# Class token's keys and values folded into the rounds of a patch tokenizer; attention 0's QKV tiles directly behind them

## What is computed

```python
red = grid.mean(axis=(3, 5))                      # 9 windows, 9 patches in each
q = _ln(red, la_ln_q_g, la_ln_q_b) @ la_wq
kv = _ln(win, la_ln_kv_g, la_ln_kv_b) @ la_wkv
local_out = red + softmax(q k) v @ la_proj_w + la_proj_b
gq = _ln(cls, ga_ln_q_g, ga_ln_q_b) @ ga_wq       # class token
gkv = _ln(local_out, ga_ln_kv_g, ga_ln_kv_b) @ ga_wkv
cls_out = cls + softmax(gq gk) gv @ ga_proj_w + ga_proj_b
patch_out = local_out @ mod_w + mod_b
h = concatenate([patch_out, cls_out])             # 10 tokens
h = h + attention_0(_layernorm(h))                # 16 heads of 16, all 10 tokens
```

## Time and profile before

| | us |
|---|---|
| median of three runs | 892.69 |
| lowest and highest | 891.36, 897.75 |
| the profiled execution, its own time | 895.31 |
| its span from first to last instruction | 893.6 |
| PE busy | 744.4 (83%) |
| DVE busy | 572.6 (64%) |
| POOL busy | 383.0 (43%) |
| ACT busy | 367.8 (41%) |

### The profile page before, as it was taken

The page is one execution under the profiler, slowest core; times in us unless marked ns, Lnnn a source line. Parts: engine busy times, 40 slices in busy tenths (PEclk is TensorE's granted clock), DMA queues, the critical chain, the costliest instruction groups (busy, mean ns, idle before and its releaser), DMA issues.

```text
span 893.6 us, 13191 instructions
## 1 busy us (share of the span) xinstructions
PE 744.4 (83%) x4447; PEld 640.8 (72%) x4447; DVE 572.6 (64%) x1230; ACT 367.8 (41%) x922; POOL 383.0 (43%) x252
## 2 busy tenths in 40 slices
PE   2989999999999998984636955999999997760768
PEld 2879999999999964441536955999999996430766
DVE  1656888888878883559899652222222223899946
ACT  2466566566566466421000131444444442430132
POOL 4665764664674332048863302333333321262310
PEclk9999999999999999987766956999999997795889
DMA  8432222222220020000020046899989942200001
GB/s 259 140 123 82 83 82 82 83 82 82 82 82 1 16 89 0 1 0 0 1 95 1 24 191 257 306 328 320 325 321 329 325 181 74 91 0 0 1 1 59
DMA packets 34488, 102.75 MB, mean 115 GB/s; under 512 B 3624, under 2 KB 12152, under 8 KB 27000
## 3 DMA queue, kind: packets, MB, share of 16 engines
q1 hardware_dynamic: 31832, 94.84, 30.7%
q0 software_dynamic: 2592, 7.10, 2.1%
HBM read 95.75 MB, written 6.17 MB: 114 GB/s over the span
## 4 chain that ended last, share of the span: by engine, by line
PE 69%; DVE 21%; DMA 2%; POOL 2%; issue 2%; ACT 2%; SPq 1%; POOLq 1%; DVEq 0%; ACTq 0%
PE banks L1422 11%; PE banks L1430 10%; PE banks L282 9%; PE banks L284 9%; PE banks L283 9%; PE banks L289 7%; PE banks L295 4%; DVE a_s L1253 4%; PE banks L1152 3%; DVE a_o L1307 3%; DVE a_prod L1053 3%; DVE w_raw L1044 3%; PE banks L1176 2%; PE banks L1760 1%; POOLq L277 1%
## 5 line engine op out<-in xcount | busy, mean ns | idle before, releaser
L392 POOL TENSOR_TENSOR x_lo<-xraw,x_hi 128x640 fp32r<-128x640 f32 x81 | 129.1, 1601 | 113.7 <-ACT x_hi L386 113.7
L282 PE MATMUL banks<-wc_hi,x_hi 128*128 128x256 f32 x405 | 121.4, 300 | 18.6 <-POOL x_lo L392 13.1
L1520 ACT ACTIVATE hid<-banks,b 128x128 f32<-128x128 f32 x216 | 79.3, 367 | 109.5 <-PE banks L1422 109.3
L284 PE MATMUL banks<-wc_hi,x_lo 128*128 128x256 f32 x405 | 116.4, 287 | 0.0
L283 PE MATMUL banks<-wc_lo,x_hi 128*128 128x256 f32 x405 | 116.4, 287 | 0.0
L282 PEld LDWEIGHTS banks<-wc_hi,x_hi 128*128 128x128 f32 x405 | 79.3, 196 | 21.4 <-issue 13.3
L1679 DVE TENSOR_TENSOR res<-banks,xb 128x256 f32<-128x256 f32 x27 | 11.5, 425 | 127.0 <-PE banks L1430 127.0
L1176 PE MATMUL banks<-ident,a_prod 128*128 128x128 f32 x372 | 51.3, 305 | 42.8 <-POOL a_prod L1053 42.8
L327 POOL TENSOR_TENSOR rstd<-veps,mhalf 128x5 f32<-128x5 f32 (+5 forms) x33 | 38.7, 1173 | 108.5 <-DVE veps L345 89.7
L1176 PEld LDWEIGHTS banks<-ident,a_prod 128*128 128x128 f32 x372 | 51.4, 221 | 44.6 <-POOL a_prod L1053 26.8
L283 PEld LDWEIGHTS banks<-wc_lo,x_hi 128*128 128x128 f32 x405 | 79.3, 196 | 2.1 <-issue 0.2
(11 more groups left out here) (270 smaller groups left out, 1828.9 us busy)
## 6 DMA issues: line engine op xcount, KB each, us to landing
w_raw<-in_w SPq DMA_DIRECT2D x28, 1024.0 KB, 7.1
xraw<-in_x_main SPq DMA_DIRECT2D x27, 768.0 KB
w1more<-in_w SPq DMA_DIRECT2D x13, 1024.0 KB, 5.7
w2more<-in_w SPq DMA_DIRECT2D x13, 1024.0 KB, 8.9
xraw<-in_x_rest SPq DMA_DIRECT2D x27, 114.0 KB
yl<-y_rows SPq DMA_DIRECT2D x2, 1028.0 KB, 7.1
a_w<-in_qkv_w SPq DMA_DIRECT2D x2, 768.0 KB, 5.6
x_rows<-w_raw SPq DMA_DIRECT2D x5, 256.0 KB, 2.0
```

The costliest lines, as they stand in the source:

```text
L282: pe.matmul(dst, a[0], b[0], start=start, stop=False)
L284: return pe.matmul(dst, a[1], b[0], start=False, stop=stop)
L392: pool.tensor_tensor(x_lo[:, k, :], xraw[:, k].rearrange("p c b -> p (c b)"), x_hi[:, k, :], ALU.subtract).then_inc(sem("x_lo_made"), 1)
L1520: act.activation(hid[:, s % 2, fc, :], bank(fc % 2, 0, P), ACT.Gelu, bias=b1[:, bass.ds(e * FC + fc, 1)]).then_inc(sem("gelu_made"), 1)
```

## The change

The norm of a local output is linear but for its inverse deviation. So gamma is multiplied into the value half of w_gkv, the column mean is subtracted from the weights, and the class query is multiplied into the key half, which leaves one column for each of 8 heads. All of it stands beside w_mod in one matrix w_mg of 256 + 256 + 8 columns. `project_mod(n)` then gives token n, the class token's values (`copy_gv`) and its eight scores (in `token_out`), both scaled by the inverse deviation of local output n (`local_std` on POOL). The matrix is prepared in rounds 0 and 1 (`class_pe`, `class_act`, `class_dve`), the class norm at the start. `turn_g`, `project_g`, `norm_g`, `affine_g` and `copy_gkv` are gone, and QKV tile 0 follows round 8. x_hi and x_lo become rings of 8, xn one of 4 in the memory of wkv_raw. `split_bias` moves into the last round. The late work of windows 7 and 8 moves between other tiles and scores.

The diff, cut to its core:

```diff
-            mm_rows(pe, bank(7), localT[:, n % 2, :], w_mod, 0, C).then_inc(sem("mod_done"), 1)
+            mm_rows(pe, bank(7, 0, 2 * C), localT[:, n % 2, :], w_mg, 0, 2 * C)
+            mm_rows(pe, bank(6, 0, H8), localT[:, n % 2, :], w_mg, M8, MG).then_inc(sem("mod_done"), 1)
+        def copy_gv(act, n):
+            act.wait_ge(sem("mod_done"), n + 1)
+            act.wait_ge(sem("local_rstd_made"), n + 1)
+            act.activation(gv_sb[:, n, :], bank(7, C, 2 * C), ACT.Identity, scale=rstd[1][:, n + 1:n + 2]).then_inc(sem("gv_made"), 1)
         def token_out(dve, n):
-            dve.wait_ge(sem("mod_done"), n + 1)
+            dve.wait_ge(sem("gv_made"), n + 1)
             dve.tensor_tensor(h_at(n), bank(7), rows[:, C:2 * C], ALU.add).then_inc(sem("patch_made"), 1)
+            dve.tensor_scalar(sc_g[:, n * H8:(n + 1) * H8], bank(6, 0, H8), rstd[1][:, n + 1:n + 2], None, ALU.mult)\
+               .then_inc(sem("weights_used"), 1)
             dve.wait_ge(sem("patch_made"), n + 1)
             tile_stats(dve, "attention 0", n, h_at(n))
+        def local_std(pool, n):
+            pool.wait_ge(sem("local_var_made"), n + 1)
+            pool.tensor_tensor(rstd[1][:, n + 1:n + 2], veps[1][:, n + 1:n + 2], mhalf[:, 0:1], ALU.pow)\
+                .then_inc(sem("local_rstd_made"), 1)
...
         def turn_agg(pe, n):
             pe.wait_ge(sem("agg_made"), 2 * (n + 1))
             if n >= 1:
-                pe.wait_ge(sem("localT_made"), n)
-            pe.wait_ge(sem("redT_made"), CH * min(n + 2, NW))
+                pe.wait_ge(sem("weights_used"), n)
+            if n < NW:
+                pe.wait_ge(sem("redT_made"), CH * min(n + 2, NW))
...
+        def class_pe(pe, n, k):
+            if (n, k) == (0, 2):
+                pe.wait_ge(sem("prep_copied"), 1)
+                pe.wait_ge(sem("redT_made"), CH)
+                turn(pe, bank(6), cls_n).then_inc(sem("prep_done"), 1)
+            if (n, k) == (0, 3):
+                pe.wait_ge(sem("prep_copied"), 1 + CH)
+                pe.wait_ge(sem("q_made"), 1)
+                mm_rows(pe, bank(7), cls_T, w_gq, 0, C).then_inc(sem("prep_done"), 1)
+            if (n, k) == (0, 5):
+                pe.wait_ge(sem("prep_made"), 1)
+                for dst, w, a, b in ((bank(7), w_gkv, C, 2 * C), (bank(7, C, C + H8), w_mg, M8, MG)):
+                    for c in range(CH):
+                        last = pe.matmul(dst, gb_col[:, c * P:(c + 1) * P], w[:, c, a:b], start=(c == 0), stop=(c == CH - 1))
+                last.then_inc(sem("prep_done"), 1)
+            if (n, k) == (0, 7):
+                pe.wait_ge(sem("prep_made"), 2)
+                turn(pe, bank(6), gvb).then_inc(sem("prep_done"), 1)
+            if (n, k) == (0, 8):
+                pe.wait_ge(sem("prep_copied"), 3 + CH)
+                mm_rows(pe, bank(7), cls_T, w_gproj, 0, C).then_inc(sem("prep_done"), 1)
+            if (n, k) == (1, 3):
+                pe.wait_ge(sem("prep_made"), 3)
+                pe.wait_ge(sem("q_made"), 2)
+                for c in range(CH):
+                    last = pe.matmul(bank(7, 0, MG - C), part[:, :], w_mg[:, c, C:MG], start=(c == 0), stop=(c == CH - 1))
+                last.then_inc(sem("prep_done"), 1)
+        def class_act(act, n, k):
+            if (n, k) == (0, 1):
+                act.wait_ge(sem("nmr_made"), CLASS_ROW + 1)
+                normalize(act, cls_n, rows[:, 3 * C:4 * C], 0, 1).then_inc(sem("prep_copied"), 1)
+            if (n, k) == (0, 2):
+                act.wait_ge(sem("prep_done"), 1)
+                affine(act, cls_T, bank(6), GAQ, "prep_copied")
+            if (n, k) == (0, 3):
+                act.wait_ge(sem("prep_done"), 2)
+                act.activation(gq, bank(7), ACT.Copy, scale=C ** -0.5).then_inc(sem("prep_copied"), 1)
+            if (n, k) == (0, 7):
+                act.wait_ge(sem("prep_done"), 4)
+                act.activation(cls_T, bank(6), ACT.Copy).then_inc(sem("prep_copied"), 1)
+        def class_dve(dve, link, n, k):
+            if (n, k) == (0, 2):
+                for c in range(CH):
+                    link(dve.tensor_copy(gb_col[:, c * P:(c + 1) * P], vecs[:, GAKV + 2 + c:GAKV + 3 + c].broadcast_to([P, P])))
+            if (n, k) == (0, 4):
+                dve.wait_ge(sem("prep_copied"), 2 + CH)
+                dve.wait_ge(sem("tok_w_loaded"), 96)
+                link(dve.tensor_tensor(vprod[:, 0:CH * C].rearrange("p (c n) -> p c n", c=CH), w_gkv[:, :, 0:C],
+                                       gq.unsqueeze(1).broadcast_to([P, CH, C]), ALU.mult))
+                dve.tensor_reduce(w_mg[:, :, M8:MG], vprod[:, 0:CH * C].rearrange("p (c h d) -> p c h d", c=CH, d=DH8), AX, ALU.add)\
+                   .then_inc(sem("prep_made"), 1)
+                for c in range(CH):
+                    dve.tensor_scalar(w_mg[:, c, C:M8], w_gkv[:, c, C:2 * C], vecs[:, GAKV + c:GAKV + c + 1], None, ALU.mult)
+            if (n, k) == (0, 6):
+                dve.wait_ge(sem("prep_done"), 3)
+                link(dve.tensor_copy(bias_g[:, :], bank(7, C, C + H8)))
+                dve.tensor_copy(gvb, bank(7)).then_inc(sem("prep_made"), 1)
+                link(dve.tensor_scalar(w_mg[:, 0, M8:MG], w_mg[:, 0, M8:MG], vecs[:, GAKV:GAKV + 1], None, ALU.mult))
+                dve.tensor_scalar(w_mg[:, 1, M8:MG], w_mg[:, 1, M8:MG], vecs[:, GAKV + 1:GAKV + 2], None, ALU.mult)\
+                   .then_inc(sem("prep_made"), 1)
+                link(dve.tensor_tensor(rows[:, 2 * C:3 * C], rows[:, 2 * C:3 * C], rows[:, 3 * C:4 * C], ALU.add))
+            if (n, k) == (0, 8):
+                dve.wait_ge(sem("prep_done"), 5)
+                dve.tensor_tensor(rows[:, 2 * C:3 * C], bank(7), rows[:, 2 * C:3 * C], ALU.add).then_inc(sem("prep_made"), 1)
+            if (n, k) == (1, 4):
+                dve.wait_ge(sem("prep_done"), 6)
+                for c in range(CH):
+                    dve.tensor_tensor(w_mg[:, c, C:MG], w_mg[:, c, C:MG], bank(7, 0, MG - C), ALU.subtract).then_inc(sem("prep_made"), 1)
...
+                class_pe(pe, n, k)
+                class_act(act, n, k)
+                    copy_gv(act, n - 2)
-                inverse_std(pool, *batch_of("class", 0))
+                local_std(pool, n - 2)
+                    local_std(pool, n - 2)
+                class_dve(dve, link, n, k)
+                    split_bias(dve)
...
+            pe.wait_ge(sem("summed"), NJ)
+            pe_start_attention(pe, 0)
+            def meanwhile(half_tile):
+                if half_tile == 0:
+                    pe.wait_ge(sem("key_used"), NJ)
                     turn_agg(pe, NW - 2)
+                if half_tile == 1:
                     project_agg(pe, NW - 2)
+                if half_tile == 3:
                     turn_local(pe, NW - 2)
+                if half_tile == 4:
                     project_mod(pe, NW - 2)
+                if half_tile == 11:
                     turn_agg(pe, NW - 1)
+                if half_tile == 12:
                     project_agg(pe, NW - 1)
+                if half_tile == 14:
                     turn_local(pe, NW - 1)
+                if half_tile == 15:
                     project_mod(pe, NW - 1)
+            for t in range(NW - 1):
+                project_tile(pe, 0, t, t + 1 < NW - 1, meanwhile)
+            turn_x(pe, 0, NW - 1)
+            project_tile(pe, 0, NW - 1, False)
+            turn_agg(pe, NW)
+            pe.wait_ge(sem("aggT_copied"), NW + 1)
+            pe.wait_ge(sem("patch_made"), NW)
+            mm_rows(pe, bank(7), aggT, w_gproj, 0, C).then_inc(sem("proj_done"), 1)
             turn_x(pe, 0, NW)
             project_tile(pe, 0, NW, False)
...
         def act_end(act):
             normalized_scales(act, "attention 0", 0)
             norm_x(act, 0, 0)
             norm_x(act, 0, 1)
+            for t in range(NW - 1):
                 copy_xT(act, 0, t)
+                if t + 2 == NW - 2:
+                    normalized_scales(act, "attention 0", 1)
+                if t + 2 < NW - 1:
                     norm_x(act, 0, t + 2)
                 if t == 0:
+                    copy_aggT(act, NW - 2)
                 if t:
                     copy_qkv(act, 0, t - 1)
                 if t == 1:
+                    exponent(act, NW - 1)
                 if t == 2:
+                    copy_localT(act, NW - 2)
                 if t == 3:
+                    copy_gv(act, NW - 2)
+                if t == 6:
+                    copy_aggT(act, NW - 1)
+            copy_qkv(act, 0, NW - 2)
+            copy_localT(act, NW - 1)
+            copy_gv(act, NW - 1)
+            normalized_scales(act, "attention 0", 2)
+            norm_x(act, 0, NW - 1)
+            copy_xT(act, 0, NW - 1)
             copy_qkv(act, 0, NW - 1)
+            exponent(act, NW)
+            copy_aggT(act, NW)
             normalized_scales(act, "attention 0", 3)
             norm_x(act, 0, NW)
             copy_xT(act, 0, NW)
...
```

(45 more changed lines are left out.)

193 lines of the change are left out of this document (54 added, 139 removed).

## The result

The changed kernel takes 916.97 us, median of four runs (915.55 to 917.78), against 894.11 for the kernel before in four runs beside it: a ratio of 1.024, interval 1.0207 to 1.0272. It is slower. The profiled execution of after is the one of 915.55 us, its fastest, 20.2 us above the 895.31 of before.

What follows compares the result with a forecast made beforehand. It took full PE to bound the rounds and the order of waits attention 0: first turn -3.4, stage +18.7, clock +8.4 make +23.7 us on 895.31, moved to the median 916.4 us; range 902.7 to 924.

Steps and rivals of the forecast that it cites:

- Rounds: On PE, full in the rounds: the wider w_mod product and 8 more columns add 1.33 us to each round from 2.
- Preparation in rounds 0 and 1: The class token's extra turns and products on the full PE add 4.4 us in rounds 0 and 1.
- Start: DVE's class row shift meets POOL's x_lo ahead of split_xT_lo(0), with PE waiting behind it: 2.4 us.
- First turn: Attention 0's first turn stands behind round 8's work on DVE and comes at 356.95 us, only 3.4 us earlier.
- The stage: From attention 0's first turn to the last scores, the order of waits adds 18.7 us.
- PE's sum: At the stage's end, PE's sum of tile 7's column follows tile 9 and takes 7.1 us.
- (b): After tile 7: ACT's copies of that tile and localT, mod(8), gv, done 40.8 us behind the first turn.
- (c): h(8), norm, tile 8, then ACT's copies and class exponent, until 49.8 us; DVE stands at weigh(9) for 6.5 us.
- (e): POOL's 8 blocks hold up tile 9's power; tile 9, sum, POOL's 9 blocks and reduction follow, ending at 102.2 us.
- The clock: PE idles before tiles 0, 8 and 9 and restarts at the 1.2 GHz level: 3 x 2.8 = 8.4 us.
- Rival 1: The clock holds over PE's gaps in attention 0: 908.0 us, chance 0.17.
- Rival 3: Attention 0 is bound by work, not order; if DVE's waits closed, the kernel takes 864.8 us, chance 0.05.

Runs made afterwards that it cites:

- e6: Changed kernel without the value half of the product with w_mg (512 back to 256 columns) and without the product of 8 columns: 905.95 us.
- e5: Changed kernel without the product of 8 columns behind each product with w_mg: 913.24 us.
- g1: Kernel before, with the order of all four queues laid out anew from the first turn of attention 0 on: 882.39 us, ratio to before 0.9859.
- e7: Changed kernel with DVE's shift for tiles 0 to 6 ahead of the last key products and lower_scores of window 8: 913.93 us.
- f4: Changed kernel with DVE's shift for tiles 0 to 6 also ahead of the two aggregations of window 7: 908.81 us.
- e2: Changed kernel with ACT's localT and gv copies of window 8 ahead of tile 7's copies, class token's exponent ahead of tile 8's: 906.41 us.
- e8: Changed kernel with POOL's power for tile 9 ahead of its blocks of tile 7's and tile 8's columns: 910.21 us.
- e3: Changed kernel with PE's waits ahead of tiles 0, 8 and 9 filled with 6, 3 and 20 unread products of 512 columns: 910.97 us.
- e1: Changed kernel with PE's sum of tile 7's column moved ahead of tile 9: 914.79 us.
- f2: Changed kernel with all four queues reordered from the last round on, and the class row's shift out of the start: 875.27 us, ratio to before 0.9773.
- e4: Changed kernel with DVE's class row shift moved from ahead of split_xT_lo(0) to the end of step 0 of round 0: 912.33 us.
- f3: Changed kernel with the edits of e2, e8 and e4 together: 899.82 us, ratio to before 1.0052.

## Why the prediction was right

The forecast was 916.4 us with the order of waits as the cause, and 916.97 were measured. That the two agree to 0.6 us is in part luck. The forecast was 23.7 us above before; the medians of four lie 22.9 apart and the profiled executions 20.2, and in the traces the last reduction ends at 464.45 us, 3.1 us earlier than the laid-out 356.95 + 102.2 + 8.4. The cause and the sizes of the steps are what was right. Its terms, each beside what the runs gave:

- **Rounds.** 1.33 us a round were forecast, for seven of them 9.3; e6 measured 9.04, and 1.31 a full round. The 8 columns at 0.47 us were 0.43 to 0.46 (e5). The price was taken from a row of the same form, and it held.
- **Preparation in rounds 0 and 1.** 4.4 us forecast. The first products with w_q of rounds 0 and 3 lie 98.28 us apart in before (53.60, 151.88) and 104.23 in after (55.39, 159.62). Of these 5.95 us one product of a round is 1.3: 4.6 to 4.7.
- **Start.** 2.4 us forecast, 1.94 at the first key split and 1.79 at the first w_q, within the bounds of 0.8 and 2.4. The mechanism, the lost port, is the row at 48.18 us with its 1.48 us. But before's profiled execution had itself lost 1.5 us to the clock here: g1, the same text, takes 5.84 us from its first nmr to the first w_q, before 7.37 and after 9.23. Against g1 the start costs 3.4 us, port and clock together, and the clock's part was not in the forecast.
- **First turn.** 356.95 forecast, 356.04 measured: 4.3 us earlier than before instead of 3.4. e7 and f4 show that it was DVE's queue that held it: the last project_kv ends at 350.1 us, 5.9 us ahead of the turn, of which f4 takes away 4.9; the 1.05 us that PE still waits there end with norm_x on ACT. The closeness owes something to chance, for before's class stage had lost 1.5 us to the clock; against g1 the stretch from w_q to turn shrinks by 4.4 us and not by 6.1.
- **The stage.** Without the clock 102.2 us were laid out; 108.41 less the 7.5 of the clock is 100.9. The step that was mis-sized is PE's sum, 6.3 us instead of 7.1: the row it was taken from is a sum into 128 columns (7.23 us), and this one goes into 112, which in proportion gives 6.3. The rest is 0.5. Of the waits, (b) and (c) were right (e2: 9.5 us come back with the two swaps on ACT), (e) was right (e8: 5.1 at nmr, with 4.7 expected).
- **The clock.** 3 x 2.8 = 8.4 us forecast, 1.9 + 2.9 + 2.7 = 7.5 measured (e3, e1). Tile 0 cost less, as its clock rose within the tile: its second half took the usual 1.13 us. Rival 1, that the clock holds, falls. The full price at all three tiles is one outcome among several: in f4 tile 8 took 1.2 us less than in after behind the same gap.
- **Rival 3, the other side.** The work of DVE was put at 57 us from the first turn, and the rival forecast 864.8 us if its waits closed. In the changed kernel they didn't. The work itself was sized rightly: DVE is busy for 57.7 us from the first turn to the last reduction of after. f2 shows the rival's condition made nearly true by hand: 78.4 us for the stage and 875.3 in all. DVE is busy for 67.2 us of these and idle for 11.3. Some 4 of the 9.5 us more are work that stood ahead of the turn in after (an aggregation and lower_scores of window 8), most of the others products and shifts that POOL held up: five blocks took 5.31 us instead of 1.48, and one column 2.02 instead of 0.16. So the rival's 59 us for the stage weren't to be had.

What the prediction didn't see is small: the clock at the start, and DVE meeting POOL at the end. The sum and POOL's 9 blocks could not simply be read as 6.3 us that one move gives back: e1 shows that DVE's last product stood close behind them.

## What to carry to other kernels

When a stage of work is removed, ask which instruction of each in-order queue stood behind it, and what that one waits for now: here the first turn of attention 0 followed the last project_kv by 5.9 us instead of 27.1, but the additions ahead of it ate 16.9 of the 21.2 us, and it came only 4.3 us earlier; the stage behind it grew by 17.4 us of waits and wider products and 7.5 us of clock; and four calls moved gave back 17. A cheap instruction on a nearly idle engine (a power, an exponent, a copy) that stands behind a long product can set the pace of a stage; move it ahead of whatever isn't needed yet. And compare a change with its own best order on both sides (f2 with g1), for otherwise one measures the order and calls it the change.

## What the runs showed of the hardware

- DVE and POOL hold each other up in both directions, and a short instruction waits for the rest of a long one: 1 column on DVE took 1.48 us behind POOL's x_lo, 1 column on POOL 2.58 us behind DVE's 8 blocks, and 10 blocks on DVE 7.76 us after POOL had started 0.02 us earlier. These are DVE's instructions with two operands in SBUF. Its reductions run on: that of 9 blocks took 2.55 us in after with POOL idle (461.90) and 2.55 us in e8 beside POOL's product (441.83).
- The granted clock isn't fixed by the program's text alone. before and g1 are the same text up to the first turn. At the start PE restarts at 48.57 in before behind a gap of 2.18 us, and at 50.77 in g1 behind 2.17; to the first w_q it takes 5.03 us in before, whose granted clock from 50.2 to 52.0 us is 0.50, the 1.2 GHz level, and 3.51 in g1, whose clock stays at 1.00. e4, f3 and f2, with a gap of 2.19 us there, take 3.50. In the class stage w_gq and the first w_gkv took 1.66 and 2.85 us in before and 1.10 and 1.88 in g1, and that is 1.5 of the 1.7 us by which g1's first turn comes earlier. PE in before, then in g1_before_orders:

```profile
336.40 1.66 PE L289 MATMUL banks<-w_gq,wc_raw 128*128 128x256 f32 x4 [1.26 <-ACT wc_raw L360]
338.28 2.85 PE L289 MATMUL banks<-w_gkv,wc_raw 128*128 128x512 f32 x4
...
337.10 1.10 PE L289 MATMUL banks<-w_gq,wc_raw 128*128 128x256 f32 x4 [1.27 <-ACT wc_raw L360]
338.26 1.88 PE L289 MATMUL banks<-w_gkv,wc_raw 128*128 128x512 f32 x4
```

  A term of the size of one such stretch can go either way between executions.
- PE's strided sum hardly feels the clock: behind 14.04 us without work its 32 records took 6.9 us in e1 (437.35 to 444.24), at granted clock 0.50 until 442 us and 0.67 behind it; behind tile 9 they took 6.3 us in after (450.25 to 456.60) at 1.00. The first half of tile 9 took 3.78 us behind its gap, 1.98 without one.
